# Cross-attention and feed-forward block: attention scores as three products of halves, single buffers of k, q and mask, another order of the first loads, and the last tile's y and h transposed on TensorE

## The chip, the cores and the metric

The kernel runs on one core of a Trainium2 chip. The metric is the device time of one execution in microseconds. The engines are TensorE (PE; its weight loads are shown as PEld), VectorE (DVE), ScalarE (ACT), GpSimd (POOL) and SyncE (SP, which here only issues DMAs).

## What is computed

Sixteen batches b, each with x of 112 rows by 512 and a context of 375 rows by 512, 16 heads of 32 columns:

```python
def _w8a8_linear(x, w, b):            # rows of x and of w rounded to 127 levels
    qx, sx = _dyn_quant(x); qw, sw = _quant_weight(w)
    return einsum('bnc,oc->bno', qx, qw) * (sx * sw[:, 0]) + b
q = _w8a8_linear(layernorm(x), wq, bq)
k = cond @ wk.T + bk                  # float32, not rounded
v = cond @ wv.T + bv
scores = einsum('bhnd,bhld->bhnl', q, k) / sqrt(32) + mask
o = einsum('bhnl,bhld->bhnd', softmax(scores), v)
x = x + _w8a8_linear(o, wo, bo)
# feed-forward on the 1792 rows, again rounded to 127 levels:
h = gelu(quant(layernorm(x)) @ quant(W1).T * scales + B1)      # 2048 wide
out = x + quant(h) @ quant(W2).T * scales + B2
```

## The kernel before

Every engine runs its own list of units, written out by hand as a string (`PE_ORDER`, `DVE_ORDER`, `ACT_ORDER`, `POOL_ORDER`, `SP_ORDER`), one letter a unit; each engine takes its letters strictly in that order, and semaphores hold the engines together. So a unit whose input is late stops everything behind it on its engine.

Attention goes by batch b. Units of PE: `k` (128 channels g of k for the whole context, 12 matmuls of 376 columns: for each of 4 pieces of the contraction the products hi·hi, lo·hi and hi·lo of float32r halves of context and wk), `v` (125 context rows, 12 matmuls of 512 columns), `q` (16 bf16 matmuls into one bank), `S` (scores of the four heads of a group g: each head contracts over 32 partitions, so the four matmuls sit in four row groups of the array and write four PSUM banks `ps_s`; operands float32, and each matmul appears twice in the trace), `T` (one third of the transpose of a head's probabilities), `P` (probabilities times v for four heads), `g` (gather of a batch's output), `x` (a row of scales broadcast by a transpose). There are 64 `S`, four a batch.

Feed-forward goes by tiles t of 128 rows (14 of them, so they straddle the batches): `o` (output projection, 4 matmuls), `u` (16 matmuls of 512 columns), `d` (16 matmuls into one bank). All are bf16.

Results of `q`, `k`, `v`, `g`, `o`, `u`, `d` go through a ring of two PSUM banks (`RING = 2`): a unit may start only when the unit two places before it in the ring has been read out. ACT reads out k (L553, writing `k_sb` with its bias) and v, DVE q, o, u and d. `T`, `P` and `x` go through two other banks. `q_sb`, `k_sb`, `v_sb` and `mask_in` have two buffers, by b % 2.

For a head DVE adds the mask and takes the maximum (L701), ACT takes the exponential (L566) and copies the transposed probabilities (L576). DVE also normalizes and rounds x, o, y and h, and at the start rounds all weights (`b`: wq and wo, L615 to L632; `w`: W1 and W2, L642 to L666; `a`: the low halves of wk and wv, L607). POOL makes low halves of the context (L440), the reciprocal square roots (L452 to L457), scale and bias of q (L484), and the second half of the rounding of h (L512, L514).

Rounded y and h are transposed by DMA from SBUF to SBUF (L401, L406): `yqT` and `hT` are what `u` and `d` of a tile start from.

SP issues the loads in the order consts (bq, bk and three rows broadcast to all partitions), context of batch 0, wq, x of batch 0, the four quarters of wk, wo, a quarter of W1, the four quarters of wv, and so on. ACT issues mask and residual loads. ACT scales bq (L540) when all five constants are there (`act.wait_ge(c_in, 16 * 5)`), and only then begins its halves of the context.

## Time and profile before

| | us |
|---|---|
| median of 3 runs | 665.77 (662.05 to 667.06) |
| the profiled execution, its own time | 667.01 |
| its span | 665.2 |
| PE busy | 609.9 (92% of the span) |
| DVE busy | 465.5 (70%) |
| ACT busy | 431.6 (65%) |
| POOL busy | 300.1 (45%) |
| mean granted TensorE clock | 0.976 |

The times are of the whole program on the device; the span runs from the first to the last instruction of the profiled execution, and 1.8 us of its time lie outside. Busy is the union of an engine's instructions. A matmul's shown length holds its latency; what one costs in a row of them is the distance between starts.

### The profile page before, as it was taken

What the parts mean: (1) busy time and instruction counts of PE and PEld (TensorE: products, weight loads), DVE (VectorE), ACT (ScalarE), POOL (GpSimd) and SP (SyncE); (2) the same over time, 40 slices, a digit from 0 to 9 for tenths busy, and PEclk for the clock granted to TensorE, in tenths of its full rate; (3) what the DMA queues carried; (4) which work ended last, traced back from release to release, by engine and by line L of the source; (5) the groups of instructions that cost most, each with busy time, mean ns of one, the idle gap of its engine ahead of it and who ended that gap; (6) DMA issues with size and microseconds to landing.
All of it is one profiled execution on the core that took longest, in us unless ns stands there. A gap on an engine that the chain in (4) does not pass through costs nothing.

```text
span 665.2 us, 14584 instructions
## 1 busy us (share of the span) xinstructions
PE 609.9 (92%) x4967; PEld 453.4 (68%) x5006; DVE 465.5 (70%) x1101; ACT 431.6 (65%) x1088; POOL 300.1 (45%) x555
## 2 busy tenths in 40 slices
PE   0899999999999999999999999999999999998553
PEld 0787878786677768777777788678777777765211
DVE  1867887979887687578697555675676774767762
ACT  2448596767758677476777686875777776677310
POOL 3474236166646555463738342462626161130431
PEclk9999999999999999999999999999999999997776
DMA  8944277533433223222322321143123212102122
GB/s 275 375 102 140 75 224 223 166 96 92 66 91 88 42 79 77 77 64 63 90 68 79 72 64 44 42 93 87 33 56 89 54 36 49 31 9 58 30 56 47
DMA packets 85816, 59.88 MB, mean 90 GB/s; under 512 B 63232, under 2 KB 73216, under 8 KB 85104
## 3 DMA queue, kind: packets, MB, share of 16 engines
q1 hardware_dynamic: 79664, 48.92, 28.5%
q10 hardware_dynamic: 6080, 10.03, 4.8%
q8 instruction: 41, 0.67, 0.4%
q14 instruction: 31, 0.25, 0.1%
HBM read 40.90 MB, written 3.67 MB: 67 GB/s over the span
## 4 chain that ended last, share of the span: by engine, by line
PE 85%; DVE 6%; DMA 3%; issue 3%; ACT 2%; POOL 1%; SPq 0%; ACTq 0%; DVEq 0%; POOLq 0%
PE ps_ring L888 20%; PE ps_ring L873 20%; PE ps_t L908 12%; PE ps_ring L964 8%; PE ps_s L899 7%; PE ps_ring L952 7%; PE ps_t L921 6%; PE ps_ring L835 2%; DMA probs<-in_wq 2%; PE ps_ring L941 2%; PE ps_ring L931 1%; DMA hT<-h_q 1%; DVE cols L775 1%; DVE h L770 1%; DMA yqT<-y_q 1%
## 5 line engine op out<-in xcount | busy, mean ns | idle before, releaser
L908 PE MATMUL ps_t<-ident,probs 112*125 112x112 f32 x768 | 182.5, 270 | 3.3 <-ACT probs L566 2.6
L701 DVE CUSTOM_DVE_ANT_0 probs<-ps_s,mask_in 112x375 f32<-112x375 f32 x256 | 127.4, 544 | 67.1 <-PE ps_s L899 55.8
L566 ACT ACTIVATE probs<-probs,neg_max 112x375 f32<-112x375 f32 x256 | 153.4, 602 | 21.3 <-DVE neg_max L701 20.8
L576 ACT ACTIVATE pT<-ps_t 125x336 f32<-125x336 f32 x256 | 112.7, 448 | 76.3 <-PE ps_t L908 74.5
L908 PEld LDWEIGHTS ps_t<-ident,probs 112*125 112x125 f32 x768 | 135.9, 189 | 27.4 <-issue 12.4
L873 PE MATMUL ps_ring<-ctx_hi,wk_hi 128*128 128x376 f32 x256 | 98.6, 385 | 17.9 <-DVE wk_lo L607 17.9
L873 PE MATMUL ps_ring<-ctx_lo,wk_hi 128*128 128x376 f32 x256 | 96.1, 375 | 0.0
L873 PE MATMUL ps_ring<-ctx_hi,wk_lo 128*128 128x376 f32 x256 | 95.5, 373 | 0.0
L888 PE MATMUL ps_ring<-wv_hi,ctx_hi 128*125 128x512 f32 x192 | 84.7, 441 | 0.7 <-ACT v_sb L559 0.5
L888 PE MATMUL ps_ring<-wv_hi,ctx_lo 128*125 128x512 f32 x192 | 83.7, 436 | 0.0
L888 PE MATMUL ps_ring<-wv_lo,ctx_hi 128*125 128x512 f32 x192 | 83.2, 433 | 0.0
L440 POOL TENSOR_TENSOR ctx_lo<-ctx_in,ctx_hi 128x376 fp32r<-128x376 f32 x64 | 62.6, 999 | 39.0 <-ACT ctx_hi L546 38.9
L964 PE MATMUL ps_ring<-w_q,hT 128*128 128x512 bf16 x213 | 55.3, 409 | 19.9 <-DMA hT<-h_q 18.7
L770 DVE SCALAR_TENSOR_TENSOR h<-ps_ring,cols,b_row 128x512 f32<-128x512 f32 x56 | 41.8, 749 | 38.1 <-PE ps_ring L952 35.6
L873 PEld LDWEIGHTS ps_ring<-ctx_hi,wk_hi 128*128 128x128 f32 x256 | 49.1, 192 | 22.8 <-DVE wk_lo L607 17.9
L899 PE MATMUL ps_s<-k_sb,q_sb 32*112 32x376 f32 x512 | 58.4, 525 | 0.0
L952 PE MATMUL ps_ring<-w_q,yqT 128*128 128x512 bf16 x205 | 53.2, 395 | 4.5 <-DMA yqT<-y_q 2.1
L553 ACT ACTIVATE k_sb<-ps_ring,bk_col 128x376 f32<-128x376 f32 x64 | 36.6, 571 | 28.9 <-PE ps_ring L873 27.8
L964 PEld LDWEIGHTS ps_ring<-w_q,hT 128*128 128x128 bf16 x224 | 22.4, 104 | 47.6 <-DMA hT<-h_q 19.7
L873 PEld LDWEIGHTS ps_ring<-ctx_lo,wk_hi 128*128 128x128 f32 x256 | 49.2, 192 | 1.7 <-issue 0.9
L873 PEld LDWEIGHTS ps_ring<-ctx_hi,wk_lo 128*128 128x128 f32 x256 | 49.1, 192 | 1.5 <-issue 1.0
L921 PE MATMUL ps_t<-pT,v_sb 125*32 125x112 f32 x1536 | 48.2, 264 | 1.5 <-ACT pT L576 1.4
(113 smaller groups left out, 1022.6 us busy)
## 6 DMA issues: line engine op xcount, KB each, us to landing
ctx_in<-in_ctxT SPq DMA_DIRECT2D x32, 375.0 KB, 3.3
h<-in_w2T SPq DMA_DIRECT2D x4, 1024.0 KB, 6.1
b_row<-in_w2T SPq DMA_DIRECT2D x4, 1024.0 KB, 5.9
xres<-in_x ACTq DMA_DIRECT2D x14, 256.0 KB, 2.8
x_in<-in_x SPq DMA_DIRECT2D x16, 224.0 KB, 2.9
...
mask_in<-in_mask ACTq DMA_DIRECT2D x16, 164.1 KB, 2.4
...
```

What stands on the lines that cost most here:

```text
L440: nc.gpsimd.tensor_tensor(ctx_lo[:, b % 2, i, :], ctx_in[:, i, :], ctx_hi[:, b % 2, i, :].bitcast(FP32), ALU.subtract).then_inc(ctx_lo_s, 1)
L566: nc.scalar.activation(probs[:, hd % SP_RING, :], probs[:, hd % SP_RING, :], ACT.Exp, scale=-1.0, bias=neg_max[:, b % 2, hd:hd + 1], accum ...
L576: nc.scalar.activation(pT[0:LR, hd % PT_RING, :], att_bank("T", b, hd, 0)[0:LR, 0:LC * N], ACT.Copy).then_inc(pT_s, 1)
L701: nc.vector.tensor_tensor_reduce(out=probs[:, hd % SP_RING, :], in0=ps_s[hd % HG][0:N, 0:L], in1=mask_in[:, b % 2, :], scale=-1.0, scalar= ...
L770: nc.vector.scalar_tensor_tensor(out=h[:, j * C:(j + 1) * C], in0=bank_of("up", t, j, 0)[:, :], scalar=y_sc[:], in1=b1_row[:, j * C:(j + 1 ...
L873: last = nc.tensor.matmul(bank[:, 0:LP], w_half[:, k, cols], x_part[:, p, k, :], start=(step == 0), stop=(step == 3 * KC - 1))
L888: last = nc.tensor.matmul(bank[0:LR, :], x_part[:, p, k, rows], w_half[:, k, :], start=(step == 0), stop=(step == 3 * KC - 1))
L899: last = nc.tensor.matmul(ps_s[j][0:N, 0:LP], q_sb[rows, b % 2, g, :], k_sb[rows, b % 2, g, :], start=True, stop=True)
L908: last = nc.tensor.transpose(att_bank("T", b, hd, 0)[0:LR, lc * N:(lc + 1) * N], probs[:, hd % SP_RING, lc * LR:(lc + 1) * LR], ident[0:N, ...
L921: last = nc.tensor.matmul(bank[D * j:D * (j + 1), 0:N], v_sb[0:LR, b % 2, lc * C + hd * D:lc * C + (hd + 1) * D], pT[0:LR, hd % PT_RING, l ...
L952: last = nc.tensor.matmul(bank_of("up", t, j, 0)[:, :], yqT[:, k, :], w1_q[:, k, j * C:(j + 1) * C], start=(k == 0), stop=(k == KC - 1))
L964: last = nc.tensor.matmul(bank_of("down", t, 0)[:, :], hT[:, k, :], w2_q[:, k, :], start=(k == 0), stop=(k == FK - 1))
```

## The change

Three things are changed, and all five orders are written anew.

1. Scores. q is written by DVE to `q_f`, scaled there by POOL, copied to float32r `q_hi` by ACT (unit `q` of ACT), and POOL writes `q_lo = q_f - q_hi` (unit `z`). ACT writes `k_hi`, and DVE writes `k_lo` from the same PSUM bank (unit `K`, 64 of them); the bank is free after DVE's. `S` becomes three passes of four matmuls in float32r: q_hi·k_hi, q_lo·k_hi, q_hi·k_lo. k, q and mask have one buffer each, so a batch's k, q and mask may be written only when the batch before has used them.
2. Start. The three broadcast rows leave `consts` for a unit `rows` with a semaphore of its own; SP's order begins with two small constants, the context of batch 0, wk, x, wv, and only then wq, wo, the rows and W1. `bq` waits for two constants.
3. End. For the last tile y and h are transposed by PE (bf16, 4 and two times 8 transposes, through ring banks) and copied to `yqT` and `hT` by DVE and ACT.

Between the first and the last `S` PE's order holds 720 `k` matmuls where it held 672, 504 `v` for 540, 52 `o` for 48, 741 `T` for 747, 15 `x` for 14; `u`, `d`, `P`, `q`, `g` are as many. Ahead of the first `S` stand 48 `k` and 72 `v` (before: 96 and 36). From the first `S` of batch 0 to the first of batch 3, PE's order holds 24 `k`, 11 `v`, 16 `u`, 8 `d` and 4 `o` matmuls more than before, and DVE's 12 `K`, 4 `u`, 2 `h`, 1 `H`, 2 `m`, 2 `Q`, 1 `y` and 1 `o` more.

```diff
--- before.py
+++ after.py
 PE_ORDER = (
-    "kkkkkkkkkkkkkkkkkkkkkkkkkkkkkkkkkkkkkkkxkkkkkkkkkOvvvvvvvvvvvvvvvvvvvvvvvvvvvvvkkkkkkkkkvvkkkvvvvvqkkkkkkkkkkkkk"
...
-    "dddTTTTTTSPooooTTTTTTTTTTTTPTTTTTTTTTPguuuuuuuuuuuuuuuuoooodddddddddddddddduuuuuuuuuuuuuuuudddddddddddddddd"
+    "kkkkkkkkkkkkkkkkkkkkkkkkkkkkxkkkkkkkkkkkkkkkkkkkkvvvvvvvvvvvvvvvvvvvvvvvvvvvvvvvOvvvvvvvvvvvvvvvvvvvvvvvvvvqvvvv"
+    "vvvvvvvvvvvSkkkkkkkkkkTkTkTTTTSkkTkTkTkkTkTkTkTkTkTkSxkkkkTkTkTkTkTkTkTkTkTSPkkTkTkTkTkTkTkkTkTqkTkTTTPPMTTTTTTT"
...
+    "TkTkTkTkkkkkkkkkkTkTkuuuuPuuuuuuuuSuuuuvTvvvvvvTvTvTvTvTvTvTvTvTvvvvPvvvvvSTTTddgddddddTTTTTTddddddddTTTTTTSPTTT"
+    "TTTooooSTTTTTTPTTTTTTTTTTTTPTTTTTTTTTPguuuuuuuuuuuuuuuuooooddddddddYdddddddduuuuuuuuuuuuuuuuHddddddddHdddddddd"
 )
 DVE_ORDER = (
-    "baaaanbbbbbbaaaaRbbbbwwwnqbRSSSSSSSSwSSSSwqnSSSSwwwwwwwwgSSSSoSSSSwwSSSSRwSSSSwnwwqRgSSSSwwwSSSSwoSSSSwwSSSSwqny"
...
+    "aaaanaaaKKaRbKbKbbbbbbbbbwwwqnbSSSSKSSSSRSSSSKwSSSwKSnKqwwwwwSSSSwSSSSwgSSSSowwwSSSSKKRwKwKqnwwgwwwSSSSwoSSSSwww"
...
 )
 ACT_ORDER = (
-    "mmrbAAAAWWWWkkkWxWkWWOvAAAAvkvAAAAkkxkEEETETTTvEEPEETTETEvTTETEPETTkTmPEEETkTTxPkkEEvTTEEATETEEPTvEATATETEvTEPEA"
...
+    "mrbAAAAWWWWWkWWWkxkkvvAAOvAAvvAAAAqvEEEkTTEETETEkTxEETETEkTPEETETEmTkTAPEPATTATTAxPqvEEvTTEEETTETEPETETTEEkTTETk"
...
 )
 POOL_ORDER = (
-    "rllllnXllllnqllXllqnlllXlnqllXllqnrybllXrbllyHqnXHqnyrblllXlHqnXyrblllqlnHXnlllrybqlXHnyrblllqlXHnyrblllqlXHnXll"
...
+    "llllnXrllllqlzlllnXnqlzlllXqnzllllrybXllllnqHzyrbXqnHzXllllqnXznqyrbXHllllnyrzbXqHnXyrbzllllHqnXryzbllllqnHXryzb"
...
 )
 SP_ORDER = (
-    "cCCQxWWWWQ1WWWW1CC1tXxCCtC1XxC2po22CXx2C22CXx2Cpo2BpoYCXxYCHHXxHHpoYCXCxHHpoXxYCCHHXpoxCYCXxHHpoYCCXxHHpoYCCXHxH"
...
+    "cCCWWWWxWWWWQQR1C1C1xXtCCtCC1xXCC2po22xX2222CpoC2BYxpoCXCHHYxXHHxXCCpoxXYxpoXHHCCYxXHHpoxYCXCHHxpoYCCXHHxpoYCCXH"
...
+        ident_bf = ident[:].bitcast(BF16).rearrange("p (c two) -> p c two", two=2)[:, :, 1]
...
-        q_sb = sb("q_sb", [P, 2, KC, N])
-        k_sb = sb("k_sb", [P, 2, KC, LP])
+        q_f = sb("q_f", [P, KC, N])
+        q_hi, q_lo = sb("q_hi", [P, KC, N], FP32R), sb("q_lo", [P, KC, N], FP32R)
+        k_hi, k_lo = sb("k_hi", [P, KC, LP], FP32R), sb("k_lo", [P, KC, LP], FP32R)
...
-        mask_in = sb("mask_in", [N, 2, L])
+        mask_in = sb("mask_in", [N, L])
...
             def consts():
                 sp.dma_start(bq_col[:], bq).then_inc(c_in, 16)
                 sp.dma_start(bk_col[:], bk).then_inc(c_in, 16)
-                sp.dma_start(bv_row[:], bv.partition_broadcast(N)).then_inc(c_in, 16)
-                sp.dma_start(bo_row[:], bo.partition_broadcast(P)).then_inc(c_in, 16)
-                sp.dma_start(b2_row[:], b2.partition_broadcast(P)).then_inc(c_in, 16)
+
+            def rows():
+                sp.dma_start(bv_row[:], bv.partition_broadcast(N)).then_inc(rows_in, 16)
+                sp.dma_start(bo_row[:], bo.partition_broadcast(P)).then_inc(rows_in, 16)
+                sp.dma_start(b2_row[:], b2.partition_broadcast(P)).then_inc(rows_in, 16)
 
             def wqo_T(i):
...
-                    nc.gpsimd.tensor_scalar(q_sb[:, b % 2, m, :], q_sb[:, b % 2, m, :], sq_col[:, m:m + 1], bq_col[:, m:m + 1],
-                                            ALU.mult, ALU.add).then_inc(q_s, 1)
+                    nc.gpsimd.tensor_scalar(q_f[:, m, :], q_f[:, m, :], sq_col[:, m:m + 1], bq_col[:, m:m + 1],
+                                            ALU.mult, ALU.add).then_inc(q_full, 1)
+
+            def q_low(b):
+                pool.wait_ge(q_hi_s, b + 1)
+                wait_for(pool, scores, KC * b)
+                nc.gpsimd.tensor_tensor(q_lo[:], q_f[:], q_hi[:].bitcast(FP32), ALU.subtract).then_inc(q_s, 1)
...
-                wait_for(act, masked, H * (b - 1))
-                act.dma_start(mask_in[:, b % 2, :], mask[b]).then_inc(mask_in_s[b % 2], 16)
+                wait_for(act, masked, H * b)
+                act.dma_start(mask_in[:], mask[b]).then_inc(mask_in_s, 16)
...
-                act.wait_ge(c_in, 16 * 5)
+                act.wait_ge(c_in, 16 * 2)
...
             def k(b, g):
                 act.wait_ge(k_pe, KC * b + g + 1)
-                wait_for(act, scores, KC * (b - 1))
+                wait_for(act, scores, KC * (b - 1) + g + 1)
                 if b == 0 and g == 0:
-                    act.wait_ge(c_in, 16 * 5)
-                nc.scalar.activation(k_sb[:, b % 2, g, :], bank_of("k", b, g, 0)[:, 0:LP], ACT.Identity,
-                                     bias=bk_col[:, g:g + 1]).then_inc(k_s, 1)
+                    act.wait_ge(c_in, 16 * 2)
+                nc.scalar.activation(k_hi[:, g, :], bank_of("k", b, g, 0)[:, 0:LP], ACT.Identity,
+                                     bias=bk_col[:, g:g + 1]).then_inc(k_hi_s, 1)
+
+            def q_high(b):
+                act.wait_ge(q_full, KC * (b + 1))
+                wait_for(act, scores, KC * b)
+                nc.scalar.activation(q_hi[:], q_f[:], ACT.Copy).then_inc(q_hi_s, 1)
...
+            def h_T():
+                act.wait_ge(hT_pe[1], 1)
+                act.wait_ge(down_pe, TILES - 1)
+                nc.scalar.activation(hT[:, 8:16, :].rearrange("p k n -> p (k n)"),
+                                     bank_of("h_T", 1)[:, :].bitcast(BF16), ACT.Copy).then_inc(hT_s[1], 1)
...
-                wait_for(dve, scores, KC * (b - 1))
-                nc.vector.tensor_tensor(q_sb[:, b % 2, :, :], bank_of("q", b)[:, 0:KC * N].rearrange("p (k n) -> p k n", k=KC),
+                wait_for(dve, q_s, b)
+                nc.vector.tensor_tensor(q_f[:], bank_of("q", b)[:, 0:KC * N].rearrange("p (k n) -> p k n", k=KC),
+            def k_low(b, g):
+                dve.wait_ge(k_hi_s, KC * b + g + 1)
+                nc.vector.scalar_tensor_tensor(out=k_lo[:, g, :], in0=bank_of("k", b, g, 0)[:, 0:LP], scalar=bk_col[:, g:g + 1],
+                                               in1=k_hi[:, g, :].bitcast(FP32), op0=ALU.add, op1=ALU.subtract).then_inc(k_s, 1)
...
-                    dve.wait_ge(mask_in_s[b % 2], 16 * (b // 2 + 1))
-                nc.vector.tensor_tensor_reduce(out=probs[:, hd % SP_RING, :], in0=ps_s[hd % HG][0:N, 0:L], in1=mask_in[:, b % 2, :],
...
+            def y_T():
+                dve.wait_ge(yT_pe, 1)
+                dve.wait_ge(up_pe, 4 * (TILES - 1))
+                nc.vector.tensor_copy(yqT[:, :, :].rearrange("p k n -> p (k n)"),
+                                      bank_of("y_T")[:, 0:C // 2].bitcast(BF16)).then_inc(yT_s, 1)
+
+            def h_T():
+                dve.wait_ge(hT_pe[0], 1)
+                dve.wait_ge(down_pe, TILES - 1)
+                nc.vector.tensor_copy(hT[:, 0:8, :].rearrange("p k n -> p (k n)"),
+                                      bank_of("h_T", 0)[:, :].bitcast(BF16)).then_inc(hT_s[0], 1)
+
...
-                pe.wait_ge(q_s, KC * b + g + 1)
+                pe.wait_ge(q_s, b + 1)
                 pe.wait_ge(k_s, KC * b + g + 1)
                 wait_for(pe, masked, H * b + HG * g)
-                for j in range(HG):
-                    rows = slice(D * j, D * (j + 1))
-                    last = nc.tensor.matmul(ps_s[j][0:N, 0:LP], q_sb[rows, b % 2, g, :], k_sb[rows, b % 2, g, :], start=True, stop=True)
+                for part, (q_half, k_half) in enumerate(((q_hi, k_hi), (q_lo, k_hi), (q_hi, k_lo))):
+                    for j in range(HG):
+                        rows = slice(D * j, D * (j + 1))
+                        last = nc.tensor.matmul(ps_s[j][0:N, 0:LP], q_half[rows, g, :], k_half[rows, g, :],
+                                                start=(part == 0), stop=(part == 2))
                 last.then_inc(scores, 1)
...
+            def y_T():
+                pe.wait_ge(y_quant_s, TILES)
+                bank = ring_bank("y_T")[:, 0:C // 2].bitcast(BF16)
+                for m in range(KC):
+                    last = nc.tensor.transpose(bank[:, m * P:(m + 1) * P], y_q[:, m * P:(m + 1) * P], ident_bf)
+                last.then_inc(yT_pe, 1)
+
+            def h_T(i):
+                pe.wait_ge(h_quant_s[i], TILES)
+                bank = ring_bank("h_T", i)[:, :].bitcast(BF16)
+                for m in range(8):
+                    at = (8 * i + m) * P
+                    last = nc.tensor.transpose(bank[:, m * P:(m + 1) * P], h_q[:, at:at + P], ident_bf)
+                last.then_inc(hT_pe[i], 1)
...
+                    if j == 0 and t == TILES - 1:
+                        pe.wait_ge(yT_s, 1)
+                    elif j == 0:
+                        pe.wait_ge(yqT_in, 16 * (t + 1))
...
+                if k % (FK // 2) == 0:
+                    if t == TILES - 1:
+                        pe.wait_ge(hT_s[k // (FK // 2)], 1)
+                    else:
+                        pe.wait_ge(hT_in[k // (FK // 2)], 16 * (t + 1))
```

## Rows read from the trace of the kernel before

**Rows 1.** The page: busy time of each engine over the whole span

```profile
PE 609.9 (92%) x4967; PEld 453.4 (68%) x5006; DVE 465.5 (70%) x1101; ACT 431.6 (65%) x1088; POOL 300.1 (45%) x555
```

**Rows 2.** Windows view, stretch: length, busy PE, PEld, DVE, ACT, POOL; PEclk, DMA, GB/s

```profile
49.60:137.90 88.30, 86.99 (x812) 68.94 (x812) 72.40 (x162) 64.09 (x184) 36.33 (x65) 1.00 0.54 161
...
150.00:175.00 25.00, 23.32 (x186) 15.61 (x187) 23.00 (x47) 19.54 (x45) 18.30 (x36) 1.00 0.47 90
```

**Rows 3.** The waits view, PE's: who waited for whom, us in total, times, longest

```profile
PE ps_ring L873 <- DVE wk_lo L607: 17.9, 1, 17.9
...
PE ps_t L908 <- ACT probs L566: 2.6, 3, 1.1
```

**Rows 4.** The chain that ended last, early part: start, us, what

```profile
20.59 0.49 POOL cols L452
...
30.91 7.01 PE ps_ring L888 x29
37.92 1.55 PE ps_ring L873 x9
...
42.37 0.95 PE ps_ring L835 x16
...
49.69 0.83 PE ps_s L899 x8
```

**Rows 5.** The same chain, its end

```profile
609.42 0.83 PE ps_s L899 x8
...
611.97 0.76 DVE y L736
...
617.38 3.35 DMA yqT<-y_q
...
621.17 6.04 PE ps_ring L952 x15
...
633.13 3.29 DMA hT<-h_q
...
652.70 3.22 DMA hT<-h_q
...
655.96 5.92 PE ps_ring L964 x16
```

**Rows 6.** Timeline of the start: start, us, engine, line, what, idle before

```profile
10.38 1.94 ACT L546 ACTIVATE ctx_hi<-ctx_in 128x376 fp32r<-128x376 f32 x4 [0.78 <-DMA ctx_in<-in_ctxT]
...
28.35 0.31 PE L861 MATMUL ps_t<-ident,cols 112*128 112x112 f32 x1 [1.48 <-POOL cols L467]
...
47.28 1.70 POOL L484 TENSOR_SCALAR q_sb<-q_sb,sq_col,bq_col 128x112 f32<-128x112 f32 x4
```

**Rows 7.** Windows view of the start, columns as in group 2

```profile
0.00:5.00 5.00, 0.00 (x0) 0.00 (x0) 0.00 (x0) 1.28 (x1) 0.74 (x7) 1.00 0.52 157
5.00:10.00 5.00, 0.00 (x0) 0.00 (x0) 0.00 (x0) 0.20 (x1) 0.48 (x1) 1.00 0.79 288
...
34.00:36.00 2.00, 2.00 (x10) 1.58 (x9) 1.89 (x2) 1.99 (x5) 1.91 (x3) 1.00 0.00 0
```

**Rows 8.** Groups of instructions by line: busy us, mean ns, then idle time before

```profile
L701 DVE CUSTOM_DVE_ANT_0 probs<-ps_s,mask_in 112x375 f32<-112x375 f32 x256 | 127.4, 544 | 67.1 <-PE ps_s L899 55.8 <-PE ps_t L908 10.9
...
L440 POOL TENSOR_TENSOR ctx_lo<-ctx_in,ctx_hi 128x376 fp32r<-128x376 f32 x64 | 62.6, 999 | 39.0 <-ACT ctx_hi L546 38.9
...
L770 DVE SCALAR_TENSOR_TENSOR h<-ps_ring,cols,b_row 128x512 f32<-128x512 f32 x56 | 41.8, 749 | 38.1 <-PE ps_ring L952 35.6 <-remote 0.9
...
L596 ACT ACTIVATE h<-h 128x1024 f32<-128x1024 f32 x28 | 29.6, 1058 | 28.8 <-DVE h L770 28.0 <-DVE neg_max L701 0.6
```

**Rows 9.** Timeline of PE: one group of scores

```profile
303.25 0.90 PE L899 MATMUL ps_s<-k_sb,q_sb 32*112 32x376 f32 x8
```

**Rows 10.** Windows view of L899 alone: how many of its instructions are in flight

```profile
303.66:303.68 0.02, 0.02 (x8) 0.00 (x0) 1.00 1.22 230
```

**Rows 11.** The page, DMA issues: count, KB each, us from issue to landing

```profile
mask_in<-in_mask ACTq DMA_DIRECT2D x16, 164.1 KB, 2.4
```

More of the change, by code:

```diff
@@ L51 @@
 PE_UNITS = {
-    "M": ("w_max", each(2)),
+    "M": ("w_max", each(2)), "Y": ("y_T", each()), "H": ("h_T", each(2)),
     "O": ("so", each()), "x": ("x_row", each(B)),
@@ L59 @@
     "a": ("w_lo", each(2, KC)), "b": ("wqo", each(2, 6)), "w": ("prepare", each(2, 14)),
-    "n": ("x_norm", each(B)), "R": ("x_recip", each(B)), "q": ("q", each(B)), "S": ("S", each(B, H)),
+    "n": ("x_norm", each(B)), "R": ("x_recip", each(B)), "K": ("k_lo", each(B, KC)), "q": ("q", each(B)), "S": ("S", each(B, H)),
     "g": ("gather", each(B)), "o": ("o_quant", each(B)), "y": ("y_res", each(TILES)), "m": ("y_norm", each(TILES)),
@@ L63 @@
     "H": ("h_quant", each(TILES)), "d": ("down", each(TILES)),
+    "Y": ("y_T", each()), "T": ("h_T", each()),
 }
@@ L66 @@
     "W": ("w_hi", each(2, KC)), "A": ("split", each(B, KC)), "k": ("k", each(B, KC)), "v": ("v", each(B, LC)),
-    "E": ("S", each(B, H)), "T": ("T", each(B, H)), "P": ("PV", each(B, KC)), "x": ("x_row", each(B)), "O": ("so", each()), "G": ("gelu", each(TILES, 2)),
-    "b": ("bq", each()), "m": ("mask_load", each(B)), "r": ("xres_load", each(TILES)), "s": ("store", each(TILES)),
+    "E": ("S", each(B, H)), "T": ("T", each(B, H)), "P": ("PV", each(B, KC)), "x": ("x_row", each(B)), "O": ("so", each()), "H": ("h_T", each()), "G": ("gelu", each(TILES, 2)),
+    "b": ("bq", each()), "q": ("q_hi", each(B)), "m": ("mask_load", each(B)), "r": ("xres_load", each(TILES)), "s": ("store", each(TILES)),
 }
 POOL_UNITS = {
-    "l": ("split", each(B, KC)), "n": ("x_scale", each(B)), "X": ("x_quant", each(B)), "q": ("q", each(B)),
+    "l": ("split", each(B, KC)), "n": ("x_scale", each(B)), "X": ("x_quant", each(B)), "q": ("q", each(B)), "z": ("q_lo", each(B)),
     "r": ("residual", each(TILES)), "y": ("y_scale", each(TILES)), "b": ("y_bias", each(TILES)),
@@ L287, in xattn_ffn_kernel @@
         x_in_s, xres_in = sem("x_in_s"), sem("xres_in")
-        mask_in_s = [sem(f"mask_in_s{n}") for n in range(2)]
+        mask_in_s = sem("mask_in_s")
         ctx_in_s = [sem(f"ctx_in_s{n}") for n in range(2)]
@@ L514, in h_quant @@
                 nc.gpsimd.tensor_scalar(half_q, half_h, -ROUND, 1.0, ALU.add, ALU.mult).then_inc(h_quant_s[1], 1)
-            units = {"split": split, "x_scale": x_scale, "x_quant": x_quant, "q": q,
+            units = {"split": split, "x_scale": x_scale, "x_quant": x_quant, "q": q, "q_lo": q_low,
                      "residual": residual, "y_scale": y_scale, "y_bias": y_bias, "h_quant": h_quant}
@@ L596, in gelu @@
                 nc.scalar.activation(part, part, ACT.Gelu_apprx_tanh).then_inc(gelu_s, 1)
-            units = {"mask_load": mask_load, "xres_load": xres_load, "store": store, "w_hi": w_hi, "bq": bq_scale, "split": split_hi, "k": k, "v": v, "S": S, "T": T, "PV": PV, "x_row": x_row, "so": so_out,
+            units = {"q_hi": q_high, "h_T": h_T, "mask_load": mask_load, "xres_load": xres_load, "store": store, "w_hi": w_hi, "bq": bq_scale, "split": split_hi, "k": k, "v": v, "S": S, "T": T, "PV": PV, "x_row": x_row, "so": so_out,
                      "gelu": gelu}
```

105 lines of the change are left out of this document (53 added, 52 removed).

## The prediction

> **What bounds the kernel now.** Read the busy times first: PE 610 of 665 us, DVE 466, ACT 432, POOL 300 [rows 1]. A mean says little, so next the stretches. From the first scores of batch 0 to the first of batch 3 (12 of the 64 `S`) PE is busy 87.0 of 88.3 us, DVE 72.4; DVE's densest 25 us are 23.0, or 92%, and there PE loses 1.7 us [rows 2]. Then PE's waits: 17.9 us for the low half of wk at the start, after that at most 2.6 in total for any one engine's unit [rows 3]. The chain of waits gives the three parts of the span: nothing on PE until 17.9; q of batch 0 at 42.4 and its scores at 49.7 [rows 4]; the last scores at 609.4; behind them a chain of single units through DVE, the DMA transposes and PE that needs 55.8 us [rows 5]. So the kernel has a start of 49.7, a middle of 559.7 in which PE's order is the bound, and an end of 55.8.
>
> **The start.** Before, ACT waits for five constants and begins the context's halves at 10.4, and four take 1.9 us [rows 6]. The queue moved 0.79 MB in the first 5 us and 1.44 MB in the next [rows 7]. Ahead of wk's last quarter now lie one mask (0.17 MB), xres (0.26), context (0.77) and wk (1.05): 2.2 MB, here at 10.0; context is in at 6.4 (1.2 MB), wk's first quarter at 7.3. ACT splits the context until 8.4, makes wk's first high half by 9.0, DVE the low one by 9.8 (both units I take at 0.7, between none and DVE's 0.75 for 512 columns, L770 [rows 8]). First matmul at 10.0, 7.9 earlier; bounds 9 to 11.5.
>
> This isn't all kept. PE's prices: `k` 0.172 (9 in 1.55), `v` 0.242 (29 in 7.01) [rows 4]. The scale row `x` waited 1.5 us before, for POOL; PE had come to it at 26.9, 39 `k` (6.7) and 2.2 us of a slow beginning after 17.9 [rows 6]. Now it stands after 28 `k`, at 10.0 + 4.8 + 2.2 = 17.0. POOL's chain from the statistics to the scale took 7.7 us (20.6 to 28.3 [rows 4, 6]); it can begin when DVE has made four low halves and x's statistics, 12.4, and ends at 20.1: a stall of 3.2 where 1.5 was. On to q of batch 0: before 42.4 - 17.9 = 24.5 us for 60 `k`, 36 `v` and 0.6 of small ones (19.6), so 4.9 over. After: 48 `k`, 57 `v` and 0.6 are 22.7; 10.0 + 22.7 + 4.9 + 1.7 = 39.3. Is wq there? wq stands behind wv now, and `R` (x's reciprocal, after 20.1) stands ahead of wq's units on DVE, where three passes over 2048 columns cost at most 9 us by L770 [rows 8]: rounded by 27 to 29. The transfers, wq's transposes among them, were all in by 34 (no byte moves from 34 to 36 [rows 7]) and the bytes ahead are the same, so 36 to 38: hidden, by the stall of `x` too; without that cover up to 3 us would show. Behind q: 0.95 on PE [rows 4], DVE's multiply 0.65, POOL's four scalings 1.7 [rows 6], ACT's `q_hi` (not in the trace; 448 elements, between nothing and the 1.06 of 1024, L596; I take 0.6), POOL's `q_lo` 1.2 (0.999 for 376 columns, L440 [rows 8]), waits 0.35. First scores at 39.3 + 0.95 + 4.5 = 44.8, against 49.7: **4.9 us gained**.
>
> **The middle, on PE.** An `S` is two passes of four matmuls: the first four start at 303.25, eight are in flight at 303.66 [rows 9, 10], and the chain books 0.83 for the eight [rows 4, 5]. So 0.41 a pass with float32, where a float32r matmul over the same 376 columns on the whole array takes 0.172. A float32r pass in row groups isn't in the trace: bounds 0.16 and 0.41; I take 0.183, nearest to `k`, the same type and columns, with 0.01 for loading four sets of weights. Three make 0.55, **0.28 less**, times 63: 17.6 us. The other letters: +48 `k` 8.3, -36 `v` 8.7, the `o`, `x` and `T` within 0.3 of each other: -0.1 in all. PE's middle: 559.7 - 17.7 = 542.0, if its idle time stays.
>
> **What is added on the other engines.** DVE gets 64 `k_lo`, from PSUM with one operand in SBUF: 0.544 by L701 (375 columns), 0.55 by L770 scaled to 376 [rows 8]; 0.56 each, 36 us. From `S` of batch 0 to that of batch 3 this is dear. PE's order there is 13.5 richer (24 `k` 4.1, 11 `v` 2.7, 28 bf16 matmuls at `v`'s 0.24 6.7) and 3.4 poorer in `S`: busy 97.1, with the same idle 98.4. DVE's gets 12 `K` 6.7, 4 `u` 3.0, two absmax and a rounding of h 5.1 (627.2 to 633.1 without the `u`), two norms and roundings of y and one residual 8.5 (from 612.0 to 617.4 a tile spends 4.9 on them [rows 5]), `o` 2.1: 72.4 + 25.4 = 97.8 us. At the 92% of rows 2 that is 106; at full share it fits. Between 0 and 8, I take **6**. It can't hide in lookahead, as before: PE's ring bank now comes free only after DVE's `K`, so PE can't run far ahead of DVE.
>
> Elsewhere DVE has cover: 466 + 36 - 98 = 404 busy in the other 550 us. A `k` bank is held 1.3 us instead of 0.7; two places on in the ring stand mostly 12 `k` (2.1) or 12 `v`, so 0.6 to 0.8 are left for the queues of two engines. Single q: `q_hi`, `q_lo` need 2 us after the last `S` of a batch. Single mask: after the last four maxima (2.2) comes the load (2.4 [rows 11]), 5.2 us in all behind the last `S` of a batch. By PE's order the first `S` of a batch stands 6.7 to 25 us behind it, but 5.3 in batch 10, and 3.7 and 3.0 in batches 12 and 13. While ACT waits to issue the mask, its exponentials and the copies of `T` are queued behind, and PE's `T` behind those. I take **3** for all of this, bounds 0 and 12. POOL (+1.2 a batch) and ACT (+0.6) have room [rows 1]. Middle: 542.0 + 9 = 551.0.
>
> **The end.** `o` of tile 12 stands ahead of the last `S`. After it DVE has the residual 1.5, four maxima 2.2, norm and rounding 3.5, the DMA 3.35 and 0.45 to `u`: 11.0 after the `S`, against 11.8 (621.2 - 609.4 [rows 5]): -0.8. y of tile 13 was hidden behind `d`; now four transposes split `d`: +0.5. h of tile 13: the rounded half is there at 652.7 and the DMA takes 3.2. Eight bf16 transposes of 128 columns: q's 16 matmuls take 0.95 [rows 4], 0.06 each, and PE is slower here (15 `u` in 6.04, 0.40 each, where `v` has 0.242 for as many columns [rows 5]), so 1.0; DVE's copy between 0.75 (the same bytes, L770) and 1.5 (twice the elements), 1.1; waits 0.3: `d` starts at 655.1, 0.9 earlier. But `H` of the other half stands behind the first eight `d` (3.2): transposes 1.0, ACT's copy 1.06 (L596), waits 0.3, all on PE's path, then eight `d` 2.7: 663.4 against 661.9, **+1.5**. End: 55.8 + 1.2 = 57.0; bounds 54.5 and 59.
>
> [...]
>
> **Sum.** 44.8 + 551.0 + 57.0 = 652.8, 12.4 under the span of 665.2. The profiled execution's own time, 667.0, is 1.2 over the median of the runs, so I take the difference from the median: 665.8 - 12.4 = 653.4, **653 us**.
>
> **Rivals.** (B) Everything fits: DVE's list at full share (-6), the small waits nil (-3), no longer stall at `x` (-2), pass 0.17 (-2.5): 640. (C) Buffers and DVE bind more: the `k` banks late by 0.1 to 0.2 us in 64 uses, or mask and q late in half of the batches: +6 to +12, 660. For it speaks that PE had almost no such waits [rows 3] only with two buffers. (D) Row groups cost each other: the four matmuls of a pass write four banks. If a float32 pass takes two steps a column, k's price makes that 0.34, and 0.41 is a fifth to a quarter more; the same on 0.172 is up to 0.22 a pass: 63 x 3 x 0.037 = +7, 660. [...] (E) Three products buy nothing, 0.28 a pass: the float32 rate is then no property of the type; 653 + 17.6 - 3 (hidden where DVE binds) = 668. (F) Slower: the pass is bound by the four row groups' reads or writes, not by the type, and stays at float32's 0.41. `S` is then 1.23, 0.68 over my price: +43, less 6 under DVE: 690. The gain is gone from 0.25 a pass on, and the kernel is over 1% slower from 0.29. Against it speaks `k`, the same type at 0.172 a matmul with 128 partitions; for it, that no float32r matmul of 32 partitions is in the trace.
>
> **How the numbers follow.** Forecast (646 to 659) 0.52; B 0.12; C 0.12; D 0.12; E 0.04; F 0.08. Range 639 to 665: it leaves out E, F and the edges of B and C. About 1% (6.7 us) is what a measurement of this kernel can tell: faster means under 659.1, which all of B, nearly all of the forecast and a third of C and D make, 0.71; slower is F, 0.08; within 1% the rest, 0.21.
>
> **What the profile after would show.** The start: first matmul near 10, a wait of PE for POOL at `x` near 17 to 20, first `S` near 45. `S`: 0.55 between its start and the next unit in the chain (F: over 1). DVE over 90% busy and PE under 97% from there to batch 3. `K` at 0.56; PE waiting for `k_lo` by name, little. The end: last `S` near 596, `d` of tile 13 in two parts with a gap of 2.4. Wrong would make it above all another price of the pass (each 0.05 is 9.5 us) and waits of PE for DVE in the middle over 15 us.

## The result and the profile after

The changed kernel takes 711.43 us (median of 4, 708.92 to 714.34) where the kernel before takes 665.81 beside it: a ratio of 1.0695, 95% interval 1.0655 to 1.0735, 46 us slower. The prediction was 653.

The page of the changed kernel, busy times and the clock that TensorE was granted in 40 slices of its 709.7 us:

```profile
PE 631.3 (89%) x5282; PEld 472.8 (67%) x5282; DVE 506.2 (71%) x1167; ACT 440.8 (62%) x1107; POOL 317.9 (45%) x571
PEclk9999999988999999999999999999998999999676
```

Beside [rows 1] PE is busier by 21 us although an `S` became cheaper, and DVE by 41. The span is 44.5 longer, so busy time accounts for half at most. The windows view (length, busy PE, PEld, DVE, ACT, POOL; PEclk, DMA, GB/s) of the two stretches of [rows 2], and then of first `S` to first `S` of batch 3, from there to the last `S`, and the end:

```profile
49.60:137.90 88.30, 80.02 (x746) 65.55 (x745) 73.02 (x156) 58.37 (x170) 32.41 (x58) 0.95 0.48 152
150.00:175.00 25.00, 19.65 (x92) 10.89 (x91) 21.51 (x42) 6.62 (x9) 16.43 (x32) 0.80 0.40 79
...
47.50:171.50 124.00, 109.37 (x929) 84.88 (x929) 101.99 (x211) 71.70 (x198) 57.38 (x103) 0.92 0.46 139
171.50:647.90 476.40, 454.64 (x4017) 346.35 (x4017) 338.11 (x852) 337.70 (x848) 221.30 (x406) 0.99 0.26 60
647.90:709.70 61.80, 35.62 (x204) 16.21 (x203) 33.78 (x62) 13.22 (x26) 16.05 (x27) 0.72 0.11 26
```

The start is 47.5, the middle 600.4, the end 61.8, against 44.8, 551.0 and 57.0 as predicted. In the middle PE is idle for 36.4 us (600.4 less 564.0); before it was 8.8, by the same view of the kernel before:

```profile
49.60:609.40 559.80, 551.03 (x4644) 413.90 (x4679) 405.48 (x1002) 401.83 (x1029) 258.48 (x483) 0.99 0.31 80
```

From the first `S` to the first `S` of batch 3 the prediction had 98.4 us and 6 for DVE; it was 124.0, with DVE busy for 102.0 of it, or 82%, where over 90% had been expected. In the densest 25 us it is 19.65 busy and the clock stands at 0.80 (granted 0.50 from 153.65 to 163.89, 1.00 in the rest), where [rows 2] shows 23.32 and 1.00 for the same stretch. PE's waits say for whom, in the form of [rows 3]:

```profile
PE ps_ring L917 <- DVE wk_lo L633: 9.5, 1, 9.5
...
PE ps_t L954 <- ACT probs L586: 6.3, 6, 2.4
PE ps_ring L987 <- DMA oqT<-o_q: 5.1, 3, 2.2
PE ps_ring L1016 <- DMA yqT<-y_q: 4.4, 4, 1.7
PE ps_ring L1016 <- DVE h L801: 3.5, 1, 3.5
PE ps_t L905 <- POOL cols L477: 3.2, 2, 1.8
PE ps_s L944 <- DVE neg_max L732: 3.0, 3, 2.5
PE ps_ring L889 <- DVE o L741: 2.4, 1, 2.4
```

The first row is the start, and two others, not shown, hold a wait of 7.1 us each for h behind the last `S`. No row of the middle is large, and hardly one names what was added: the waits for `k_lo` come to 1.6 us ahead of `k` and 1.1 ahead of other units, the one for `q_lo` is 2.1. There are many joints of a few us each, with ACT, DVE, DMA and POOL all among them. Such a list doesn't tell a cause; the experiments have to.

The timeline of one `S` of the changed kernel, beside [rows 9]:

```profile
312.21 0.44 PE L944 MATMUL ps_s<-k_hi,q_hi 32*112 32x376 f32 x4
312.48 0.34 PE L944 MATMUL ps_s<-k_hi,q_lo 32*112 32x376 f32 x4
312.65 0.34 PE L944 MATMUL ps_s<-k_lo,q_hi 32*112 32x376 f32 x4
312.92 0.91 PE L954 MATMUL ps_t<-ident,probs 112*125 112x112 f32 x6
```

From the second pass to the third it is 0.17, nearly as guessed, but 0.27 from the first to the second and 0.27 from the third to the next unit. In all an `S` takes 0.71, not 0.55: some 0.2 more than three passes of 0.17.

### The profile page after: what moved, and what is told of

Same layout as the page of the kernel before. It is cut to its first block, busy times and chain, and to the rows that moved or that the text cites. A ratio compares the mean times of both kernels' runs of the same rounds, so it can differ in the third digit from the quotient of the medians.

```text
span 709.7 us, 15311 instructions
## 1 busy us (share of the span) xinstructions
PE 631.3 (89%) x5282; PEld 472.8 (67%) x5282; DVE 506.2 (71%) x1167; ACT 440.8 (62%) x1107; POOL 317.9 (45%) x571
## 4 chain that ended last, share of the span: by engine, by line
PE 61%; DVE 19%; DMA 8%; issue 5%; POOL 3%; ACT 2%; SPq 1%; DVEq 0%; ACTq 0%; POOLq 0%
PE ps_ring L917 14%; PE ps_ring L932 12%; PE ps_t L954 8%; PE ps_ring L1030 7%; PE ps_ring L1016 6%; PE ps_s L944 5%; PE ps_t L967 4%; DVE probs L732 3%; DMA hT<-h_q 3%; DVE cols L806 2%; DMA yqT<-y_q 2%; PE ps_ring L879 2%; PE ps_ring L987 2%; DVE h_q L713 1%; DMA oqT<-o_q 1%
## 5 line engine op out<-in xcount | busy, mean ns | idle before, releaser
L917 PE MATMUL ps_ring<-ctx_hi,wk_hi 128*128 128x376 f32 x256 | 102.0, 398 | 12.0 <-DVE wk_lo L633 9.5
L917 PE MATMUL ps_ring<-ctx_lo,wk_hi 128*128 128x376 f32 x256 | 99.0, 387 | 0.0
L917 PE MATMUL ps_ring<-ctx_hi,wk_lo 128*128 128x376 f32 x256 | 98.1, 383 | 0.0
L450 POOL TENSOR_TENSOR ctx_lo<-ctx_in,ctx_hi 128x376 fp32r<-128x376 f32 x64 | 64.6, 1036 | 43.5 <-ACT ctx_hi L561 43.5
L1030 PE MATMUL ps_ring<-w_q,hT 128*128 128x512 bf16 x224 | 61.9, 424 | 12.6 <-DMA hT<-h_q 10.6
L724 DVE SCALAR_TENSOR_TENSOR k_lo<-ps_ring,bk_col,k_hi 128x376 fp32r<-128x376 f32 x64 | 38.5, 605 | 43.6 <-ACT k_hi L568 43.6
L1016 PE MATMUL ps_ring<-w_q,yqT 128*128 128x512 bf16 x224 | 58.9, 405 | 10.2 <-DMA yqT<-y_q 4.4
L579 ACT ACTIVATE v_sb<-ps_ring 125x512 f32<-125x512 f32 x48 | 28.6, 595 | 47.5 <-PE ps_ring L932 47.0
L494 POOL TENSOR_SCALAR q_f<-q_f,sq_col,bq_col 128x112 f32<-128x112 f32 x64 | 31.5, 506 | 55.2 <-DVE q_f L719 54.9
L622 ACT ACTIVATE h<-h 128x1024 f32<-128x1024 f32 x28 | 29.6, 1056 | 40.9 <-DVE h L801 40.8
L506 POOL TENSOR_TENSOR xres<-xres,bo_row 128x512 f32<-128x512 f32 x14 | 18.4, 1317 | 76.0 <-DMA xres<-in_x 76.0
L967 PE MATMUL ps_t<-pT,v_sb 125*32 125x112 f32 x1536 | 49.4, 264 | 3.0 <-ACT pT L596 2.3
```

The costliest lines, as they stand in the source:

```text
L450: nc.gpsimd.tensor_tensor(ctx_lo[:, b % 2, i, :], ctx_in[:, i, :], ctx_hi[:, b % 2, i, :].bitcast(FP32), ALU.subtract).then_inc(ctx_lo_s, 1)
L724: nc.vector.scalar_tensor_tensor(out=k_lo[:, g, :], in0=bank_of("k", b, g, 0)[:, 0:LP], scalar=bk_col[:, g:g + 1], in1=k_hi[:, g, :].bitca ...
L917: last = nc.tensor.matmul(bank[:, 0:LP], w_half[:, k, cols], x_part[:, p, k, :], start=(step == 0), stop=(step == 3 * KC - 1))
L967: last = nc.tensor.matmul(bank[D * j:D * (j + 1), 0:N], v_sb[0:LR, b % 2, lc * C + hd * D:lc * C + (hd + 1) * D], pT[0:LR, hd % PT_RING, l ...
L1016: last = nc.tensor.matmul(bank_of("up", t, j, 0)[:, :], yqT[:, k, :], w1_q[:, k, j * C:(j + 1) * C], start=(k == 0), stop=(k == KC - 1))
L1030: last = nc.tensor.matmul(bank_of("down", t, 0)[:, :], hT[:, k, :], w2_q[:, k, :], start=(k == 0), stop=(k == FK - 1))
```

## The experiments

Medians are of each kernel's own runs; the ratios are to runs of the kernel before on the same chip, which stood at 663.9 to 665.5. About 1% can be told.

**The parts that can be done alone.** The start, in the old lists:

```
SP    cCCQxWWWWQ1WWWW...   ->  cCCWWWWxWWWWQQR1...    (R: the three rows)
DVE   baaaanbbbbbbaaaaR... ->  aaaanaaaaRbbbbbbbbbbb...
PE    39 k, x, 9 k         ->  28 k, x, 20 k
```

> The kernel before with the change's start alone: context and wk first in SP's list, the three rows that are read late behind wq and wo, DVE's eight low halves ahead of the wq stages, PE's `x` after 28 steps of `k`; everything from the first S on as before. The changed kernel had its first matmul 7.9 us earlier, and its first S only 2.1 us earlier, with POOL's longer q ahead of it. Theory A (the start is a gain that the changed kernel spends elsewhere): first S 2 to 5 us earlier, 661 to 664 us against 665.8. Theory B (what comes behind sets the time, the head start is used up in waits): 665 to 667. Theory C (the start is itself a part of the loss, since wq's stages and the first q come later): above 668.

Measured: 667.3, ratio 1.0017 [0.9985, 1.0049]. Its timeline of PE (idle before in brackets):

```profile
11.31 0.68 PE L880 MATMUL ps_ring<-ctx_hi,wk_hi 128*128 128x376 f32 x1 [11.31 <-DVE wk_lo L614]
...
22.17 0.31 PE L868 MATMUL ps_t<-ident,cols 112*128 112x112 f32 x1 [2.87 <-POOL cols L474]
...
31.08 1.11 PE L860 MATMUL ps_ring<-ident,so_col 128*128 128x128 f32 x4 [3.61 <-DVE so_col L625]
...
52.95 0.90 PE L906 MATMUL ps_s<-k_sb,q_sb 32*112 32x376 f32 x8
```

The first matmul comes 6.6 us earlier, the first `S` 3.3 later than in [rows 4]: `so` now waits for DVE's later wq and wo stages, a wait that the changed kernel's own list avoids, and TensorE's granted clock was 0.50 for 10.2 us between 23.5 and 37.1, where the kernel before had 1.00 up to its first `S`. The time is theory B's. So this edit in the old lists is no gain and no part of a 46 us loss; what an earlier first `S` is worth it can't show, since it has a later one. The last tile alone:

```
PE    oooo d*16 u*16 d*16  ->  oooo d*8 Y d*8 u*16 H d*8 H d*8
```

> The kernel before with the last tile's y and h transposed by PE alone. The changed kernel needed 6.0 us more than before from its last S to the end; the prediction put this edit at +1.2. If the transposes by PE and their evictions are the cause, the end grows by 5 to 6 us and the time is 671 to 672. If the prediction's terms hold, 667. If the changed kernel's longer end comes from its work left over and from the slow clock, this kernel is within 1.5 us of 665.8.

Measured: 665.3, 0.9993 [0.9971, 1.0016]; from its last `S` (604.60) to the end of its span (660.8) are 56.2 us, against 55.8. The rows of its end:

```profile
648.20 1.03 PE L989 MATMUL ps_ring<-ident,h_q 128*128 128x128 bf16 x8 [7.07 <-DVE h_q L706]
650.02 3.59 PE L1015 MATMUL ps_ring<-w_q,hT 128*128 128x512 bf16 x8 [0.79 <-DVE hT L824]
653.41 1.06 PE L989 MATMUL ps_ring<-ident,h_q 128*128 128x128 bf16 x8
655.59 1.90 PE L1015 MATMUL ps_ring<-w_q,hT 128*128 128x512 bf16 x8 [1.12 <-ACT hT L609]
```

The predicted 1.0 us for eight transposes is right: 1.03 and 1.06, both at a granted clock of 0.50. A single one has a shown length of 0.31 (0.29 the first), but in a row they start 0.11 apart, and that is what each adds. The whole edit is worth nothing either way, +0.4 for the predicted +1.2. So the 4.8 us by which the changed kernel's end is too long do not come from this edit as it stands in the old lists.

**The products.** Three passes, and one pass, in the old lists:

```
q_sb, k_sb: FP32 -> FP32R
for part in range(3):            # one pass: without this loop
    matmul(ps_s[j], q_sb[rows, b % 2, g, :], k_sb[rows, b % 2, g, :],
           start=(part == 0), stop=(part == 2))
```

> The kernel before with q_sb and k_sb declared as rounded float32 and each S made as three passes over the same q_sb and k_sb, which leaves the low halves out of the computation; orders, buffers and side work as before. It prices the products alone. The trace of the changed kernel books 0.70 us for an S against 0.83: that gives 63 x 0.13 = 8.2 us less, 657 to 659. The prediction's 0.55 us would give 648. If PE has its slack taken by other engines anyway, 663 to 666. If products of four row groups are dear in themselves (rival F), above 670.

> The kernel before with q_sb and k_sb declared as rounded float32 and one pass for each S (the low halves are left out of the computation). With the three-pass kernel at 657.7 it gives the price of a pass and of what an S has besides its passes. If a pass costs 0.17 and the rest of an S 0.20, S is 0.37 and 63 of them save 63 x 0.46 = 29 us against before: 637, or 10.3 us a pass. If the prediction's 0.183 a pass with nothing besides were right, S would be 0.18 and the time 625. If PE is not the bound once S is short, 645 to 655.

Measured: three passes 657.7, 0.9869 [0.9829, 0.9909]; one pass 649.4, 0.9786 [0.9752, 0.9820]. One `S` and the unit behind it, first of the three-pass kernel, then of the one-pass kernel:

```profile
299.94 0.77 PE L900 MATMUL ps_s<-k_sb,q_sb 32*112 32x376 f32 x12
300.64 0.36 PE L910 MATMUL ps_t<-ident,probs 112*125 112x112 f32 x1
```

```profile
123.76 0.43 PE L899 MATMUL ps_s<-k_sb,q_sb 32*112 32x376 f32 x4
124.12 0.36 PE L908 MATMUL ps_t<-ident,probs 112*125 112x112 f32 x1
```

So an `S` is 0.36 with one pass, 0.70 with three, 0.83 in float32: 0.17 a pass and 0.19 that it costs once. Three passes give 63 x 0.13 = 8.2 us, and 7.9 arrived, as expected. Of the 29.6 us of one pass (63 x 0.47) about half arrived, 14.6: PE's middle, in the windows view, is busy for 25 us less than before, but idle for 10 more (544.3 less 525.7 are 18.6), so with short `S` PE's order is no longer the only bound:

```profile
49.24:593.57 544.33, 525.69 (x4392) 407.60 (x4424) 406.56 (x1002) 401.33 (x1029) 259.50 (x483) 0.99 0.32 82
```

The one-pass kernel is the fastest of this study. It keeps only the first of the three products, so its scores are coarser.

**The new lists alone.**

```
changed kernel, with: S, q_sb[2], k_sb[2], mask_in[2] and their waits as before
lists: the changed ones, less the letters K (DVE), z (POOL), q (ACT)
```

> The changed kernel with its lists of order, its start and its end, but the scores, the two buffers of q, k and mask, and the evictions as in the kernel before (float32 S; the letters of k_lo, q_hi and q_lo dropped from the lists). It prices the new lists with none of the new work and none of the single buffers. Theory of the lists (the in-order lists themselves put engines' work behind late waits, so that PE stands and its clock falls): 690 us or more, near the changed kernel's 711 plus 8 for the float32 S. Theory of side work and buffers: 664 to 672, and the 45 us come back as soon as k_lo, q_hi, q_lo and the single buffers are put in. Between them, 672 to 690, both have a share.

Measured: 705.5, 1.0601 [1.0556, 1.0646]. This is the finding: with not one instruction of the new products and not one buffer fewer, the lists cost 40 us, together with the new start and end, which were worth nothing in the old lists. The middle of this kernel and two of its stretches:

```profile
45.60:644.50 598.90, 559.50 (x4654) 416.27 (x4690) 407.62 (x1003) 402.34 (x1032) 261.55 (x494) 0.99 0.30 76
150.00:175.00 25.00, 20.24 (x108) 12.02 (x110) 19.18 (x40) 8.70 (x17) 15.30 (x32) 0.93 0.40 97
175.00:200.00 25.00, 21.46 (x200) 16.28 (x200) 14.58 (x40) 21.27 (x49) 9.34 (x20) 0.93 0.22 48
```

PE is idle for 39.4 us of it, 30.6 more than before, and busy for 8.5 more, for a sum of work that is equal by the prediction's prices. Of the idle time 21.3 us lie ahead of 200, where it was 3.2 before. In 175 to 200 no engine is at its limit, ACT at 85% the nearest beside PE, and PE stands for 3.5 us. Its waits are the changed kernel's almost row for row (the ACT row 5.9 and 6.3, yqT 4.6 and 4.4, `neg_max` 3.0 and 3.0, `o` 2.4 and 2.4):

```profile
PE ps_t L938 <- ACT probs L577: 5.9, 6, 2.4
PE ps_ring L1000 <- DMA yqT<-y_q: 4.6, 5, 1.7
PE ps_ring L971 <- DVE h L787: 3.4, 1, 3.4
PE ps_ring L971 <- DMA oqT<-o_q: 3.1, 1, 3.1
PE ps_s L929 <- DVE neg_max L718: 3.0, 3, 2.5
...
PE ps_ring L875 <- DVE o L727: 2.4, 1, 2.4
```

Is one engine the reason? Two kernels take work away from the engine that PE waits for, one of them with a control:

```
DVE: maxima and scalings of w1, w2 over [:, 0:512] of 2048
ACT: Exp over probs[:, hd % SP_RING, 0:L // 2]
```

> The kernel of the changed lists alone (705.5) with DVE's preparation of w1 and w2 shortened: their eight maxima and eight scalings go over 512 of 2048 columns, which leaves the rest of the weights unscaled. It takes some 20 us from DVE, all of it before 130 us. If the new lists lose their time there because DVE, loaded with the preparation, answers late (u, o and q wait for it in the trace), the time falls by 10 to 20 us, to 685 to 695, and most of that between the first S and the 16th. If the lists lose by their own order, whatever DVE's load, it stays above 700.

> The same shortening in the kernel before, as the control: PE lost only 7 us up to the 16th S there, so the time falls by at most 5 us, to 661 to 665, whichever theory holds for the new lists. If it falls by 10 or more, DVE binds the kernel before too and the comparison with the new lists says little.

> The kernel of the new lists alone (705.5) with ACT's exponential over 187 of the 375 columns of each head, which leaves the others as the masked scores; ACT has some 60 us less to do. PE's waits in the new lists name ACT with 12.6 us, DVE with 12, DMA with 11. If a late ACT is what the lists lose by, 690 or less. If the loss is spread over many joints of lists that no longer mesh, each engine's share small: 699 to 704.

Measured: 702.9, 1.0595 [1.0530, 1.0660], for DVE in the new lists; 664.3, 1.0013 [0.9991, 1.0035], in the old; 704.4, 1.0594 [1.0553, 1.0636], with half of ACT's exponential. That took 18 us from DVE's busy time, and 40 from ACT's exponential, not 60 (603 ns for 375 columns, 446 for 187). Both bring 1 to 3 us, within what can't be told, and beside the kernel before nothing (1.06 all three). So neither DVE's preparation of the weights nor ACT's exponential is what the lists lose by; the loads of POOL and of the DMA queue, and each list by itself, weren't tried.

**Single buffers and side work in the new lists.**

```
changed kernel without K, z, q_hi; k_hi and mask_in single, q_hi two buffers
products: ((q_hi, k_hi),) * 3
```

> The changed kernel without its side work: its lists, start and end, its one buffer of k and of mask, its three passes, but over the same q and k halves (low halves left out of the computation), with no k_lo, q_hi and q_lo; q has two buffers, as it had with q_f. The new lists with the float32 S and two buffers took 705.5. Theory A (lists, products and side work add up): the passes give back 8, so 697 to 699, and the side work costs 12 to 14 of the changed kernel's 711. Theory B (single buffers bind in the new lists): 703 or more, and the side work is worth less than 8. Theory C (the side work is what the changed kernel waits for after all): below 690.

Measured: 699.0, 1.0511 [1.0469, 1.0553]: theory A. From the kernel before to the changed one it adds up: lists +39.7 (705.5), products and single buffers -6.5 (699.0), side work +12.4 (711.4). The products' own -8 leaves 1 to 2 us for the single buffers, which is less than can be told. By the profiled executions (first `S` at 43.5, last at 638.4, end at 697.2 without the side work) it adds 4.0 to the start, 5.5 to the middle and 3.0 to the end.

**Side work in the old lists.** Low halves go to scratch there, so it fits with k and q double. `K` stands where it was ready in the three-pass trace:

```
DVE   ...nqbRSSSSSSSSwSSSSwqnSSSSwwwwwwwwgSSSS...
  ->  ...KnqbKRKKSSSSSSSSwSSSSwqnSSSSwwKwwwwKwwKgKSSSS...
ring bank of k: free at k_s (DVE) instead of ACT's eviction
```

> The kernel before, with its own lists and two buffers of q and k, the three passes over the same q_sb and k_sb (low halves left out of the computation), and all side work of the change at its size: the second eviction of every k bank by DVE, written to scratch, with the ring bank kept until it is done; ACT's q_hi; POOL's q_lo to scratch; one buffer of mask. Each new letter stands in the lists where the trace of the three-pass kernel had its engine at that time. The three-pass kernel took 657.7. Theory of the lists: the side work fits in the slack of these lists, 658 to 664. Theory of side work: DVE's 38 us of k_lo and the held ring banks cost 10 us or more, 668 to 680. The prediction had 9 us for all of it, 667.

> The kernel with the side work in the lists of before (693.3) without ACT's q_hi and POOL's q_lo; DVE's k_lo stays, with the ring bank kept until it is done, and the one buffer of mask; three passes over the same halves, low halves left out. The three-pass kernel took 657.7, so 35.6 us are to be shared out. PE's waits in the trace name k_lo with 17 us and q_lo with 9. Theory K (DVE standing in its list at k_lo until ACT has made k_hi, 49 us in sum, holds up masks and ring banks): 680 or more. Theory Q (q's longer chain ahead of each batch's first S): 672 or less.

> The kernel with the side work in the lists of before (693.3), but the ring bank of k comes free with ACT's eviction: DVE's k_lo reads k_sb twice instead of the bank (low halves left out of the computation). DVE's instruction, its place in the list and its wait for ACT stay. If the held bank is the cost, 680 or less; if it is DVE's standing and the later masks, 688 to 695.

> The three-pass kernel (657.7; the same q and k in all passes, low halves left out of the computation) with one buffer of mask and nothing else: the mask of a batch is asked for behind the last exponential of the batch before. If the mask's load stands ahead of each batch's first masked scores, some 1 to 2 us for 15 batches, 665 to 680, and k_lo cost that much less than it seemed. If there is time between the batches, 657 to 661.

Measured: all side work 693.3, 1.0462 [1.0413, 1.0512]; without the q part 687.5, 1.0337 [1.0295, 1.0378]; with the bank free early 691.2, 1.0390 [1.0355, 1.0426]; one mask buffer alone 659.4, 0.9911 [0.9881, 0.9940]. The 693.3 is above what either theory had given. The shares of its 35.6 us over the three-pass kernel are then 1.7 for the mask, 28 for `k_lo` (theory K) and 6 for q. In the kernel with all side work PE waits for `k_lo` by name ahead of `k`, `v`, `g`, `o` and `d` (the five rows sum to 17.4), and for q's chain too:

```profile
PE ps_s L921 <- POOL q_lo L496: 8.7, 4, 3.2
PE ps_ring L954 <- DVE k_lo L714: 4.9, 5, 2.2
PE ps_ring L894 <- DVE k_lo L714: 4.4, 7, 1.9
PE ps_ring L987 <- DVE k_lo L714: 3.7, 5, 1.2
PE ps_ring L909 <- DVE k_lo L714: 3.2, 5, 1.3
...
PE ps_ring L964 <- DVE k_lo L714: 1.2, 2, 0.6
```

and DVE's group by line shows the other side of the same wait (busy, mean ns, then idle before it):

```profile
L714 DVE SCALAR_TENSOR_TENSOR k_lo<-ps_ring,bk_col,k_sb 128x376 bf16<-128x376 f32 x64 | 38.7, 605 | 48.7 <-ACT k_sb L564 48.2
```

38.7 us of work, and 48.7 of standing ahead of it, with masks queued behind. With the bank free early (691.2) PE no longer names `k_lo` ahead of a ring unit, but DVE's `K`, which now reads `k_sb` twice, takes 750 ns in the mean where it took 605 with the bank and `k_sb`, 48.0 us in all (the median is 609, the longest 1373), it still stands for 42.1, and PE waits for the maxima (`neg_max`) 6.7 us. So the 2 us between the two are not the price of the held bank alone. Two kernels move `K` later:

```
e14: K at least 1.2 us behind ACT's eviction, bank held until K
e15: K at least 6 us behind, bank free at ACT's eviction (K reads k_sb twice)
```

> The kernel with the side work in the lists of before (693.3; low halves left out of the computation), each k_lo moved in DVE's list to the unit that in the three-pass trace began 1.2 us or more behind ACT's eviction. DVE then no longer stands at k_lo, but the ring bank is held longer. If DVE's standing is the cost, 670 to 680; if k_lo's place hardly matters, since DVE's work itself or the held bank costs, 688 to 698.

> The kernel with the side work and the ring bank freed by ACT's eviction (691.2; low halves left out of the computation), each k_lo 6 us behind the eviction. No bank is held and DVE need not stand; what remains is DVE's 38 us of work in a list with slack. Standing as the cost: 665 to 678. DVE's added work as the cost (masks 0.6 us later for each k_lo ahead of them): 685 or more.

Measured: 719.4, 1.0809 [1.0756, 1.0862], and 681.9, 1.0245 [1.0202, 1.0288]. The 719.4 has one run of 727.6 in it; the other three have a median of 717.0. This is outside of both expectations: moving `K` back with the bank held costs 24 us more. In the trace, which is of the run of 727.6, the same five rows of waits for `k_lo` sum to 41.0 us, where they were 17.4; the two largest:

```profile
PE ps_ring L894 <- DVE k_lo L714: 16.4, 14, 2.2
...
PE ps_ring L909 <- DVE k_lo L714: 7.7, 7, 2.1
```

DVE still stands ahead of `K` for 25.1 us, half of what it did, so this kernel doesn't separate the two costs. The held bank is dear when `K` isn't taken at once. The 681.9 lies between its two expectations: with the bank free, the later place brings 9 us. Neither of the two places that were tried with the bank held was good. Freed of both, `k_lo` still costs: 681.9 is 22 over the mask kernel, 6 of it q's if q costs there what it did above. The group by line there:

```profile
L714 DVE SCALAR_TENSOR_TENSOR k_lo<-k_sb,bk_col 128x376 bf16<-128x376 f32 x64 | 41.2, 643 | 0.0
```

No standing, 41 us of work, and some 16 us of time for it. How these 16 come about no run shows.

## Why the prediction was wrong, by its steps

**The step that failed** is the last line of "The middle, on PE": "PE's middle: 559.7 - 17.7 = 542.0, if its idle time stays". It weighed the new list of PE by its letters, found the sum equal to 0.1, and took the old list's idle time, 8.8 us, along. But that idle time was a property of how five lists meshed. In the new lists it is 39.4 with the old work (new lists alone), and PE's busy time for an equal sum of letters is 8.5 longer; 40 of the 46 us are the new lists. The "3 for all of this, bounds 0 and 12" and DVE's "6, bounds 0 to 8" were for waits with a name (ring, q, mask, DVE's share); the range had no term for the rest. One sign stood in both diffs: before, 54 of the 60 groups `k(b, g)` that could be done by then end ahead of `S(b-1, g)`; with single buffers none may. PE has less work of its own to fall back on when a transpose or a chain through DVE and DMA is late. That this is why the lists mesh worse is argued from the lists, not shown; old lists with only k's lead removed weren't tried on the chip, and which of the five lists loses the time stays open.

**DVE and the waits, +9.** The changed kernel's middle is 49.4 over the predicted 551.0. Of these 18.6 are idle time of PE (36.4, where 8.8 and the 9 had been allowed) and 30.8 busy time (564.0 for 542.0 less 8.8): 9.5 for the price of `S`, and 21.3 by which PE's other work kept it busy for longer than priced. The prediction had no term for that either. TensorE's lower clock can be 10 of it at most (last section); the rest stays open. Side work costs 12.4 in the new lists, but 5.5 of it in the middle, for which the 9 were meant. The price of `K` was nearly right (0.605 for 0.56), its place was not: in the old lists it cost 28. Rival C's "6 to 12" comes on top of the 9, 15 to 21 in all: the old lists' 36 is beyond it, the new lists' 12.4 short of it.

**`S`, 0.28 less.** The direction was right (0.70 for three float32r passes, 0.83 in float32), the size off: the pass is 0.17 (predicted 0.183), but an `S` costs 0.19 once besides, for which the prediction had no term. If float32's 0.83 holds the same 0.19, its two passes are 0.32 each, not 0.41; no float32 `S` of another length was run. So the gain is 0.13, 8.2 us instead of 17.6. The term was mis-sized by dividing a whole `S` by its passes. Rivals D and F, a dearer pass, are wrong in that, though D's `S` of three times 0.22 is nearer to the 0.70 than the forecast's 0.55. The 0.01 for loading weights was a guess, and that a float32 pass takes two steps a column, from which D had its 0.22, no run shows. Nor does one show what the 0.19 consists of that an `S` costs once, with one pass (0.36) as with three (0.70); in the changed kernel it shows as 0.27 instead of 0.17 from the first pass to the second, and again from the third to the next unit.

**The start, -4.9.** It was -2.2. The first matmul came at 9.5 (predicted 10.0), 8.4 earlier than before, and PE stood 1.8 at `x` (3.2). The first `S` was at 47.5, not 44.8: PE waited 1.0 for a `k_lo` and 2.1 for `q_lo`, for POOL's four scalings of q took 3.40, not 1.7:

```profile
42.00 3.40 POOL L494 TENSOR_SCALAR q_f<-q_f,sq_col,bq_col 128x112 f32<-128x112 f32 x4 [5.04 <-DVE q_f L719]
...
46.31 1.13 POOL L500 TENSOR_TENSOR q_lo<-q_f,q_hi 128x448 fp32r<-128x448 f32 x1
```

Without the side work the new lists have their first `S` at 43.5, so the chain of q and `k_lo` costs 4.0 here. What these few us are worth in the end no run shows: the start tried in the old lists had a later first `S`.

**The end, 57.0.** It was 61.8. The edit's own +1.2 was nearly right (+0.4 alone). With the new lists and the old work the end is 58.5, without the side work 58.8, so of the rest some 2 came with the lists and 3 with the side work, for which the end had no term.
